# A one-core transformer kernel: the attention output bias as one early row, and the first queries placed ahead of the last down products

## The chip, the cores and the metric

The kernel is one program on one core of a Trainium2 chip. Its five engines run side by side, each through its own queue in order: TensorE (PE: matmuls, with weight loads PEld overlapping them), VectorE (DVE), ScalarE (ACT), GpSimd (POOL) and SyncE (SP, which here only issues DMAs). They wait for each other by semaphores. The metric is the device time of one launch in microseconds (us), lower is better; ratios are taken on the median of several runs.

## What is computed

Two layers on x of 8 batches x 256 tokens x 256 columns, each an attention and a mixture of experts, with residual sums between (L0_xattn mixes the top 2 of 64 context rows; L0_ffn, the first experts, has 16 routed ones, top 4, and a shared one, 96 wide; L1_xattn has 16 heads over 64 context rows; L1_ffn, the second experts, has 8 of width 704, top 2). The last two lines are what the change touches of L1_xattn, with v_img = ctx @ Wv_img + bv_img; the text part of the context is empty here:

```
x = x + L0_xattn(layernorm(x))
x = x + L0_ffn(layernorm(x))
x = x + L1_xattn(layernorm(x))
x = x + L1_ffn(layernorm(x))

q = rms_norm(x @ Wq + bq, gq)
out = attend(q, k_img, v_img) @ Wo + bo
```

The value bias bv is carried past the softmax and added with bo as one row `bv @ Wo + bo`, the same for all tokens: this is "the bias row" below.

## The kernel before

Rows of x stay on the chip in `x_sb` (16 tiles of 128 tokens, two tiles to a batch). Everything is written out by hand: each engine's block lists its instructions in the order in which they run, and nothing reorders them.

**First experts.** The 12 chunks of 128 routed hidden columns and a 13th chunk of 96 shared ones (C0 = 13) are done for four groups of 512 tokens (NG = 4). For a chunk PE makes gate and up products into PSUM banks 0/1 and 2/3 (`up0`, each float32 product as three products of high and low parts, lines 1034 to 1036), ACT takes Silu of the gate (772), DVE multiplies it with the up part (1530, semaphore `b_prod`), multiplies by the tokens' routing weight out of bank 4 (1535, `b_mult`; not for the shared chunk), splits the result into a high part (1540) and a low part (1544, `b_hidden`), and PE makes the down products of the chunk into banks 6 and 7 (`down0`, 12 products for a group, `b_down`). PE runs one chunk ahead: the up products of chunk c+1 stand before the down products of chunk c. After the last group there is nothing to stand ahead, and `down0(NG - 1, C0 - 1, 1)` follows directly on the chunk before. DVE then adds banks 6 and 7 to `x_sb` (1522, `x_new`) and makes the layer norm of the batches 6 and 7: statistics (1329 to 1339), the power of -0.5 on POOL (501), and the normed rows (1350, `ln_rows`). The batches 0 to 5 were normed, turned and copied to `xnT` inside the expert loop already.

**Bias row.** SP issues the load of bo, spread over 128 partitions (`bo_rows`, 128 KB), at line 410, behind its wait for the last down products. PE adds bv @ Wo (1131, two products) and identity @ bo_rows (1132) in bank 4; ACT copies the sum back into `bo_rows` (789, `bo_ready`); POOL adds it to all of `x_sb` (591), one batch at a time.

**Queries.** For each batch b PE makes x @ Wq (1110, four matmuls, eight records in the profile, since each float32 product runs as two), ACT writes the squares and the biased queries (796, 798), and PE sums the squares over columns (1118, `squares`, into bank 7). PE does batch 0, batch 1 and the squares of 0, then turns the normed rows of the batches 6 and 7 (906), which ACT copies (680), and then a loop does the batches 2 to 7. After it DVE scales the sums (1562), POOL takes their power (595), and attention begins (scores 1151, maxima 1567, difference 1575, exponential 819).

SP's queue behind line 410 holds the loads of the second experts' weights, 18 MB (413 and 421), which are first used some 150 us later.

```python
            for n in range(2):
                sp.wait_ge(hi_out[n], 16 * (NPART // 2))
                sp.wait_ge(lo_out[n], 16 * (NPART // 2))
            sp.dma_start(bo_rows, bo1_in.partition_broadcast(P)).then_inc(in_bo, 16)
```

Of the kernel before, what the change touches and what calls it, by code (L numbers as in the profile page):

```python
# [15 lines left out]
ACT = mybir.ActivationFunctionType  # L16
AX = mybir.AxisListType

P = 128
B, S, D = 8, 256, 256  # L20
# [6 lines left out]
C0 = E0 * I0 // P + 1  # L27
# [31 lines left out]
def program(nc, x_in, ctx_in, ctxT_in, itok_in, descT_in, wq0_in, bq0_in, rw0_in, ebias_in,  # L59
            gu0_in, dn0_in, wq1_in, bq1_in, gq1_in, wk1_in, bk1_in, gk1_in, wv1_in, bv1_in,  # L60
            wo1_in, bo1_in, wg1_in, wexp_in, out_rows):
    with ExitStack() as st:
# [38 lines left out]
        arena = sb("arena", [P, 4224])  # L101

        def view(tensor, first, *shape):
            v = tensor[:, first:first + int(np.prod(shape))]
            names = "abcd"[:len(shape)]
            if len(shape) > 1:
                v = v.rearrange(f"p ({' '.join(names)}) -> p {' '.join(names)}",
                                **dict(zip(names[:-1], shape)))
            return v

        xnT = view(xmem, 0, KD, NT * P)
# [41 lines left out]
        kbd = view(wexp, last, 2, KD * HALF)  # L153
        pT = view(wexp, last + 2048, 2, 8, P)
        bo_rows = view(wexp, last + 4096, D)

        xn = view(arena, 0, 2, TB, D)
        xn2 = view(arena, 2560, 2, TB, D)
# [17 lines left out]
        sqT = view(arena, 1024, 2, KD, S)  # L176
# [34 lines left out]
        ident = sb("ident", [P, P])  # L211
        identb = sb("identb", [P, P], BF16)
        ones = sb("ones", [P, P])
# [17 lines left out]
        wq1 = sb("wq1", [P, KD, D])  # L231
# [31 lines left out]
        def bank(i, n=1):  # L263
            return ps[:, 512 * i:512 * (i + n)]
# [9 lines left out]
        b_high, b_low, b_max, b_mult = sem("b_high"), sem("b_low"), sem("b_max"), sem("b_mult")  # L274
        b_prod, b_routed, b_sig, b_silu = sem("b_prod"), sem("b_routed"), sem("b_sig"), sem("b_silu")
# [24 lines left out]
        in_bo, in_ctx, in_exp0, in_exp7 = sem("in_bo"), sem("in_ctx"), sem("in_exp0"), sem("in_exp7")  # L300
        in_gu, in_dn, in_route = [sem("in_gu0"), sem("in_gu1")], sem("in_dn"), sem("in_route")
        in_itok, in_kv, in_rest = sem("in_itok"), sem("in_kv"), sem("in_rest")
# [11 lines left out]
        bo_sum, bo_ready = sem("bo_sum"), sem("bo_ready")  # L314
# [4 lines left out]
        x_new = sem("x_new")  # L319
# [17 lines left out]
        XA, XB, XC = NT, NT + NT // 2, 2 * NT + NT // 2  # L337
        NG = NT // 4
# [17 lines left out]
        def _(sp):  # L356
# [20 lines left out]
            sp.dma_start(wq1[:, :, :], wq1_in.rearrange("(k p) n -> p k n", p=P)).then_inc(in_rest, 16)  # L377
            sp.dma_start(wo1[:, :, :], wo1_in.rearrange("(k p) n -> p k n", p=P)).then_inc(in_rest, 16)
            sp.dma_start(wg1[:, :, :], wg1_in.rearrange("(k p) n -> p k n", p=P)).then_inc(in_rest, 16)

            xn_v = xn_rows.rearrange("(t p) d -> p t d", p=P)
            sp.wait_ge(pool_fill, 1)
# [24 lines left out]
            for n in range(2):  # L407
                sp.wait_ge(hi_out[n], 16 * (NPART // 2))
                sp.wait_ge(lo_out[n], 16 * (NPART // 2))
            sp.dma_start(bo_rows, bo1_in.partition_broadcast(P)).then_inc(in_bo, 16)  # L410
            for e in range(7):
                whole = slice(e * WE, (e + 1) * WE - D)
                sp.dma_start(w_hi[:, whole].bitcast(F32), w_hi_rows[:, whole]).then_inc(in_exp0, 16)
# [262 lines left out]
        def _(act):  # L676
# [107 lines left out]
            for g in range(NG):  # L784
                silu_group(g, g)

            act.wait_ge(in_rest, 16 * 3)
            act.wait_ge(bo_sum, 1)
            act.activation(bo_rows, bank(4)[:, 0:D], ACT.Copy).then_inc(bo_ready, 1)

            def queries(b, k):
                act.wait_ge(c_q, b + 1)
                if k >= 2:
                    act.wait_ge(c_ssq, b - 1)
                for m in range(KD):
                    act.activation(sqT[:, k % 2, m, :], bank(2 + k % 2)[:, m * S:(m + 1) * S], ACT.Square,
                                   bias=vecs[:, 0, m:m + 1]).then_inc(c_sq, 1)
                    act.activation(xnT[:, m, bass.ds(b * S, S)], bank(2 + k % 2)[:, m * S:(m + 1) * S],
                                   ACT.Identity, bias=vecs[:, 0, m:m + 1]).then_inc(c_qT, 1)
            for b in range(2):  # L800
                queries(b, b)
            for b in range(B - 2, B):
                copy_batch(2, b, 0)
            with act.Fori(1, B // 2) as pair:
# [87 lines left out]
        def _(pe):  # L892
# [22 lines left out]
            for m in range(KD):  # L915
                for k in range(KD):
                    pe.matmul(bank(6)[:, m * NK:(m + 1) * NK], wq0[:, k, m * P:(m + 1) * P], descT[:, k, :],
                              start=(k == 0), stop=(k == KD - 1))
            for k in range(KD):
                mm = pe.matmul(bank(6)[0:1, 256:256 + NK], bq0[:, k:k + 1], descT[:, k, :],  # L920
                               start=(k == 0), stop=(k == KD - 1))
# [66 lines left out]
            for m in range(KD):  # L988
                for k in range(KD):
                    mm = pe.matmul(bank(6 + m), wkv[:, k, 0, m * P:(m + 1) * P], ctxT[:, k, :, 0, :],  # L990
                                   start=(k == 0), stop=(k == KD - 1))
# [62 lines left out]
            def down0(g, c, k):  # L1054

                i, rows = g * C0 + c, P if c < C0 - 1 else I0
                if c == 0 and k:
                    pe.wait_ge(x_new, g * 2 + XA)
                if k == 0 and c in (0, 4, 7, 10):
                    pe.wait_ge(dn_low_ready, (0, 4, 7, 10).index(c) + 1)  # L1060
                for j in range(4):
                    if j % 2 == 0:
                        pe.wait_ge(b_hidden, i * 2 + 1 + j // 2)
                    cols = slice(j * P, (j + 1) * P)
                    mm = in_parts(bank(6, 2)[:, j * D:(j + 1) * D], h_high[0:rows, c % 2, cols], h_low[0:rows, c % 2, cols],
                                  dn_high[0:rows, c, :], dn_low[0:rows, c, :], c == 0 and j % 2 == 0, c == C0 - 1)
                mm.then_inc(b_down, 1)
# [29 lines left out]
            pe.wait_ge(b_low, B)  # L1097
            with pe.Fori(1, NG) as g:
                ffn0_group(g, 1)
            down0(NG - 1, C0 - 1, 1)  # L1100

            def queries(b, k):
                pe.wait_ge(ln_copied, 2 * B + b + 1)
                if k >= 2:
                    pe.wait_ge(c_qT, (b - 1) * KD)
                for m in range(KD):
                    for h in range(KD):
                        mm = pe.matmul(bank(2 + k % 2)[:, m * S:(m + 1) * S], wq1[:, h, m * P:(m + 1) * P],  # L1110
                                       xnT[:, h, bass.ds(b * S, S)], start=(h == 0), stop=(h == KD - 1))
                mm.then_inc(c_q, 1)

            def squares(b, k):
                pe.wait_ge(c_sq, b * KD + KD)
                for j in range(TB):
                    for m in range(KD):
                        mm = pe.matmul(bank(7)[:, bass.ds(b * TB + j, 1)], sqT[:, k % 2, m, j * P:(j + 1) * P],
                                       ones[:, 0:1], start=(m == 0), stop=(m == KD - 1))
                mm.then_inc(c_ssq, 1)  # L1120

            def queries_squares(b, k):
                queries(b, k)
                if k == 1:
                    pe.wait_ge(x_new, XB)
                if k >= 1:
                    squares(b - 1, k - 1)
            pe.wait_ge(in_rest, 16 * 3)
            pe.wait_ge(in_bo, 16)
            for k in range(KD):  # L1130
                pe.matmul(bank(4)[:, 0:D], vecs[:, 4, k:k + 1].broadcast_to([P, P]), wo1[:, k, :], start=(k == 0), stop=False)
            pe.matmul(bank(4)[:, 0:D], ident[:, :], bo_rows, start=False, stop=True).then_inc(bo_sum, 1)
            for b in range(2):
                queries_squares(b, b)
            for b in range(B - 2, B):
                turn_rows(2, b, b % 2)
            with pe.Fori(1, B // 2) as pair:
# [678 lines left out]
```

## Time and profile before

| | |
|---|---|
| median of 3 runs | 782.27 us (781.16 to 784.03) |
| profiled execution, its own time | 782.75 us |
| its span, first to last instruction | 781.0 us |
| mean granted TensorE clock | 0.929 of full speed |
| busy: PE / DVE / POOL / ACT | 700.1 / 476.0 / 328.7 / 259.1 us |
| chain of waits that ends last, by engine | PE 75%, DVE 15%, issue 4%, ACT 2%, DMA 1% |

The span is 1.75 us shorter than the time of the same execution. PE is busy nearly throughout, so the places where it stands still, and those where its clock is at half, are the ones to read. Times in a timeline are microseconds from the start of the span. A row of the timeline may merge several instructions (x8); the square brackets give how long the engine had been idle before it and who ended that.

### The profile page before, as it was taken

What the parts mean: (1) busy time and instruction counts of PE and PEld (TensorE: products, weight loads), DVE (VectorE), ACT (ScalarE), POOL (GpSimd) and SP (SyncE); (2) the same over time, 40 slices, a digit from 0 to 9 for tenths busy, and PEclk for the clock granted to TensorE, in tenths of its full rate; (3) what the DMA queues carried; (4) which work ended last, traced back from release to release, by engine and by line L of the source; (5) the groups of instructions that cost most, each with busy time, mean ns of one, the idle gap of its engine ahead of it and who ended that gap; (6) DMA issues with size and microseconds to landing.
All of it is one profiled execution on the core that took longest, in us unless ns stands there. A gap on an engine that the chain in (4) does not pass through costs nothing.

```text
span 781.0 us, 14817 instructions
## 1 busy us (share of the span) xinstructions
PE 700.1 (90%) x4735; PEld 623.7 (80%) x4735; DVE 476.0 (61%) x1326; ACT 259.1 (33%) x491; POOL 328.7 (42%) x318
## 2 busy tenths in 40 slices
PE   4799479999999999969799992699999999999996
PEld 4668368878878878858677772589999999999996
DVE  5959956667667768760399956644444444444443
ACT  1356133222223222314567740022222222222221
POOL 6136933334334434426212115235555545455542
PEclk9786679999999999988899995599999999999998
DMA  8801046766666666559900008422254345525221
GB/s 223 312 1 53 3 139 221 246 210 221 225 233 203 216 231 225 196 169 427 337 12 32 29 29 272 160 78 41 43 156 114 77 149 157 151 48 156 43 35 21
DMA packets 60407, 115.08 MB, mean 147 GB/s; under 512 B 15200, under 2 KB 29536, under 8 KB 57920
## 3 DMA queue, kind: packets, MB, share of 16 engines
q1 hardware_dynamic: 50656, 103.61, 38.8%
q0 software_dynamic: 8736, 10.39, 8.0%
q8 instruction: 37, 0.61, 0.3%
q10 hardware_dynamic: 960, 0.33, 0.2%
q14 instruction: 18, 0.15, 0.1%
HBM read 69.02 MB, written 45.29 MB: 146 GB/s over the span
## 4 chain that ended last, share of the span: by engine, by line
PE 75%; DVE 15%; issue 4%; ACT 2%; DMA 1%; another core or an unknown queue 1%; POOLq 0%; POOL 0%; DVEq 0%; ACTq 0%
PE ps L1034 18%; PE ps L1036 17%; PE ps L1035 17%; PE ps L1277 3%; PE ps L1151 2%; PE ps L1160 2%; PE ps L1110 2%; PE ps L1197 2%; PE ps L1077 1%; DVE h_high L1540 1%; DVE h_low L1544 1%; PE ps L1173 1%; PE ps L906 1%; PE ps L1256 1%; DVE arena L1350 1%
## 5 line engine op out<-in xcount | busy, mean ns | idle before, releaser
L561 POOL TENSOR_TENSOR part_lo<-wexp,part_hi 128x512 fp32r<-128x512 f32 x68 | 89.4, 1324 | 133.5 <-ACT part_hi L783 127.1
L650 POOL DMA_INDIRECT out_rows<-vbd,slot_row x39 | 62.9, 1613 | 109.3 <-DVE vbd L1731 77.1
L1034 PE MATMUL ps<-w_hi,x_high 128*128 x312 | 104.4, 335 | 1.1 <-DVE x_low L1736 1.1
L1036 PE MATMUL ps<-w_hi,x_low 128*128 x312 | 101.0, 324 | 0.0
L1035 PE MATMUL ps<-up_low,x_high 128*128 x312 | 100.9, 324 | 0.0
L1752 DVE TENSOR_TENSOR arena<-arena,ps 128x704 f32<-128x704 f32 x39 | 34.6, 887 | 103.9 <-ACT arena L874 76.7
L1034 PE MATMUL ps<-xn_high,gu_high 128*128 (+3 forms) x208 | 92.5, 445 | 0.1
L772 ACT ACTIVATE wexp<-ps 128x512 f32<-128x512 f32 (+1 forms) x52 | 31.1, 599 | 160.2 <-PE ps L1036 160.2
L1035 PE MATMUL ps<-xn_low,gu_high 128*128 (+3 forms) x208 | 82.2, 395 | 0.0
L1036 PE MATMUL ps<-xn_high,gu_low 128*128 (+3 forms) x208 | 82.2, 395 | 0.0
L501 POOL TENSOR_TENSOR rstd<-ve,mhalf 128x2 f32<-128x2 f32 (+1 forms) x32 | 22.8, 713 | 115.3 <-DVE ve L1339 115.3
L874 ACT ACTIVATE arena<-ps 128x704 f32<-128x704 f32 x39 | 29.6, 760 | 120.8 <-PE ps L1036 65.1
L1034 PE MATMUL ps<-dn_high,h_high 128*128 128x256 f32 (+1 forms) x208 | 61.5, 296 | 7.2 <-DVE h_low L1544 7.2
L1034 PE MATMUL ps<-w_hi,hT_high 128*128 x195 | 58.8, 302 | 2.0 <-DVE hT_high L1745 2.0
L1034 PEld LDWEIGHTS ps<-w_hi,x_high 128*128 128x128 f32 x312 | 59.3, 190 | 1.5 <-issue 1.5
L1035 PEld LDWEIGHTS ps<-up_low,x_high 128*128 128x128 f32 x312 | 59.2, 190 | 0.0
L1530 DVE TENSOR_TENSOR wexp<-wexp,ps 128x512 f32<-128x512 f32 (+1 forms) x52 | 35.6, 685 | 38.6 <-ACT wexp L772 38.5
L1036 PEld LDWEIGHTS ps<-w_hi,x_low 128*128 128x128 f32 x312 | 59.0, 189 | 0.0
L1035 PE MATMUL ps<-dn_low,h_high 128*128 128x256 f32 (+1 forms) x208 | 59.0, 284 | 0.0
L1036 PE MATMUL ps<-dn_high,h_low 128*128 128x256 f32 (+1 forms) x208 | 58.8, 283 | 0.0
L1544 DVE TENSOR_TENSOR h_low<-wexp,h_high 128x256 fp32r<-128x256 f32 (+1 forms) x104 | 55.4, 573 | 1.8
L1036 PE MATMUL ps<-w_hi,hT_low 128*128 x195 | 55.7, 286 | 0.0
(274 smaller groups left out, 1700.2 us busy)
## 6 DMA issues: line engine op xcount, KB each, us to landing
wexp<-in_wexp SPq DMA_DIRECT2D x68, 256.0 KB, 3.2
w_hi_rows<-part_hi SPq DMA_DIRECT2D x68, 256.0 KB, 2.5
w_lo_rows<-part_lo SPq DMA_DIRECT2D x68, 256.0 KB, 2.1
w_hi<-w_hi_rows SPq DMA_DIRECT2D x8, 2048.0 KB, 20.2
up_low<-w_lo_rows SPq DMA_DIRECT2D x8, 1408.0 KB, 6.2
down_low<-w_lo_rows SPq DMA_DIRECT2D x8, 768.0 KB, 8.6
wexp<-in_gu SPq DMA_DIRECT2D x2, 1632.0 KB, 10.6
xn_rows<-arena SPq DMA_DIRECT2D x8, 256.0 KB, 2.1
```

What stands on the lines that cost most here:

```text
L501: pool.tensor_tensor(rstd[:, bass.ds(b * TB, TB)], ve[:, bass.ds(b * TB, TB)], mhalf[:, 0:1].broadcast_to([P, TB]), ALU.pow).then_inc(ln_r ...
L561: pool.tensor_tensor(part_lo[:, n % 2, :], part_w[:, n % 4, :], part_hi[:, n % 2, :].bitcast(F32), ALU.subtract).then_inc(p_lo, 1)
L650: pool.indirect_dma_start(out=out_rows, out_offset=bass.IndirectOffsetOnAxis(ap=slot_row[:, i:i + 1], axis=0), in_=yb[:, i % 2, :], in_off ...
L772: act.activation(sg0[0:rows, c % 2, :], bank(c % 2)[0:rows, :], ACT.Silu).then_inc(b_silu, 1)
L874: act.activation(sg1.rearrange("p (a n) -> p a n", a=2), bank(0, 2).rearrange("p (a n) -> p a n", a=2)[:, :, 0:HALF1], ACT.Silu).then_inc( ...
L1034: pe.matmul(out, high, rows_high, start=start, stop=False, skip_group_check=True)
L1035: pe.matmul(out, high, rows_low, start=False, stop=False, skip_group_check=True)
L1036: return pe.matmul(out, low, rows_high, start=False, stop=stop, skip_group_check=True)
L1277: mm = pe.transpose(bank(4, 2)[:, c * P:(c + 1) * P], h1[:, c * P:(c + 1) * P], ident[:, :])
L1530: dve.tensor_tensor(hm0[0:rows_, c % 2, :], sg0[0:rows_, c % 2, :], bank(2 + c % 2)[0:rows_, :], ALU.mult).then_inc(b_prod, 1)
L1544: dve.tensor_tensor(h_low[0:rows_, c % 2, cols], hm0[0:rows_, c % 2, cols], h_high[0:rows_, c % 2, cols].bitcast(F32), ALU.subtract).then_ ...
L1752: dve.tensor_tensor(h1[:, 0:I1].rearrange("p (a n) -> p a n", a=2), sg1.rearrange("p (a n) -> p a n", a=2), bank(2, 2).rearrange("p (a n) ...
```

## The change

It has four parts. (1) bo is loaded as one row of 1 KB into partition 96 of `arena`, near the start of SP's queue, and the 128 KB load at line 410 is gone. (2) The product of the identity with `bo_rows` becomes a product of one row of ones with `bo_row`, contracted over that single partition. (3) On PE, the queries of batch 0 and the bias products stand ahead of the last down products, and the queries of batch 1 behind them; the two PSUM banks of the queries are swapped (`3 - k % 2`), so that the queries of batch 0 go to bank 3, which the chunk before the last has left. (4) On ACT the copy of the bias row stands between the queries of batch 0 and those of batch 1.

```diff
+        bo_row = arena[96:97, 1792:1792 + D]
...
             sp.dma_start(wg1[:, :, :], wg1_in.rearrange("(k p) n -> p k n", p=P)).then_inc(in_rest, 16)
+            sp.dma_start(bo_row, bo1_in.unsqueeze(0)).then_inc(in_bo, 16)
...
-            sp.dma_start(bo_rows, bo1_in.partition_broadcast(P)).then_inc(in_bo, 16)
...
-            act.wait_ge(in_rest, 16 * 3)
-            act.wait_ge(bo_sum, 1)
-            act.activation(bo_rows, bank(4)[:, 0:D], ACT.Copy).then_inc(bo_ready, 1)
-
...
-                    act.activation(sqT[:, k % 2, m, :], bank(2 + k % 2)[:, m * S:(m + 1) * S], ACT.Square,
+                    act.activation(sqT[:, k % 2, m, :], bank(3 - k % 2)[:, m * S:(m + 1) * S], ACT.Square,
...
-            for b in range(2):
-                queries(b, b)
+            queries(0, 0)
+            act.wait_ge(bo_sum, 1)
+            act.activation(bo_rows, bank(4)[:, 0:D], ACT.Copy).then_inc(bo_ready, 1)
+            queries(1, 1)
...
             with pe.Fori(1, NG) as g:
                 ffn0_group(g, 1)
-            down0(NG - 1, C0 - 1, 1)
...
             pe.wait_ge(in_rest, 16 * 3)
+            pe.wait_ge(b_prod, NG * C0 - 1)
+            queries(0, 0)
             pe.wait_ge(in_bo, 16)
+            pe.wait_ge(b_mult, NG * (C0 - 1))
             for k in range(KD):
                 pe.matmul(bank(4)[:, 0:D], vecs[:, 4, k:k + 1].broadcast_to([P, P]), wo1[:, k, :], start=(k == 0), stop=False)
-            pe.matmul(bank(4)[:, 0:D], ident[:, :], bo_rows, start=False, stop=True).then_inc(bo_sum, 1)
-            for b in range(2):
-                queries_squares(b, b)
+            pe.matmul(bank(4)[:, 0:D], ones[96:97, :], bo_row, start=False, stop=True).then_inc(bo_sum, 1)
+            down0(NG - 1, C0 - 1, 1)
+            pe.wait_ge(b_prod, NG * C0)
+            queries(1, 1)
+            pe.wait_ge(x_new, XB)
+            squares(0, 0)
```

TensorE's queue at the end of the first experts' loop, before (the branch of line 1098 closes the loop; the first three and last three of the 12 down products are those of 1034 to 1036 in their order):

```order
L1098 COMPARE_AND_BRANCH
L1034 MATMUL ps<-dn_high,h_high 128x256 [waits b_hidden]
...
L1036 MATMUL ps<-dn_high,h_low 128x256
L1131 MATMUL ps<-wo1,vecs 128x256 [waits in_bo,in_rest]
L1131 MATMUL ps<-wo1,vecs 128x256
L1132 MATMUL ps<-wexp,ident 128x256
L1110 MATMUL ps<-xmem,wq1 128x256 [waits ln_copied]
...
L1118 MATMUL ps<-ones,arena 128x1 [waits c_sq,x_new]
```

The same place after the change (its line numbers are one or two lower):

```order
L1097 COMPARE_AND_BRANCH
L1108 MATMUL ps<-xmem,wq1 128x256 [waits ln_copied,b_prod,in_rest]
L1108 MATMUL ps<-xmem,wq1 128x256 x3
L1129 MATMUL ps<-wo1,vecs 128x256 [waits b_mult,in_bo]
L1129 MATMUL ps<-wo1,vecs 128x256
L1130 MATMUL ps<-arena,ones 128x256
L1033 MATMUL ps<-dn_high,h_high 128x256 [waits b_hidden]
...
L1035 MATMUL ps<-dn_high,h_low 128x256
L1108 MATMUL ps<-xmem,wq1 128x256 [waits ln_copied,b_prod]
L1108 MATMUL ps<-xmem,wq1 128x256 x3
L1116 MATMUL ps<-ones,arena 128x1 [waits c_sq,x_new]
```

Four query products and three bias products now stand between the loop and the last 12 down products; four query products moved behind those; the turns of the batches 6 and 7 and the loop over the other queries follow as before.

## Rows read from the trace of the kernel before

**Rows 1.** Chain of waits, 344 to 363 us: start, length, what (all in us).
```profile
344.07 0.43 DVE h_low L1544
344.50 0.04 issue
344.55 0.39 PE ps L1034
...
346.60 0.23 PE ps L1036
346.82 0.02 issue
346.84 4.15 DMA wexp<-in_bo
350.99 0.14 issue
351.12 2.04 PE ps L1131 x4
353.17 0.85 PE ps L1132 x2
354.02 4.33 PE ps L1110 x16
```

**Rows 2.** Timeline of TensorE, 342 to 364 us: start, length, instruction, idle before.
```profile
342.57 0.28 PE L1036 MATMUL ps<-dn_high,h_low 128*128 128x256 f32 x1
344.55 0.39 PE L1034 MATMUL ps<-dn_high,h_high 96*128 96x256 f32 x1 [1.69 <-DVE h_low L1544]
...
360.57 0.63 PE L906 MATMUL ps<-ident,arena 128*128 128x128 f32 x4 [0.96 <-ACT xmem L680]
361.04 1.95 PE L1110 MATMUL ps<-xmem,wq 128*128 x8
362.82 0.95 PE L1118 MATMUL ps<-ones,arena 128*128 128x1 f32 x8
363.63 1.97 PE L1110 MATMUL ps<-xmem,wq 128*128 x8
```

**Rows 3.** Timeline of TensorE, attention: a projection at full clock, scores and turns.
```profile
378.36 1.13 PE L1151 MATMUL ps<-wexp,arena 64*128 64x256 f32 x8
382.17 2.08 PE L1151 MATMUL ps<-wexp,arena 64*128 64x256 f32 x8 [2.68 <-DVE arena L1575]
384.20 1.97 PE L1160 MATMUL ps<-ident,arena 128*128 128x128 f32 x8
...
395.10 1.03 PE L1197 MATMUL ps<-wo,wexp 128*128 128x256 f32 x4
```

**Rows 4.** Timeline of VectorE, 346 to 379 us.
```profile
346.85 1.28 DVE L1522 TENSOR_TENSOR x_sb<-x_sb,ps 128x512 f32<-128x512 f32 x2 [2.02 <-PE ps L1036]
...
350.61 0.73 DVE L1350 TENSOR_SCALAR arena<-x_sb,mean,rstd 128x256 f32<-128x256 f32 x2
351.60 1.31 DVE L1350 TENSOR_SCALAR arena<-x_sb,mean,rstd 128x256 f32<-128x256 f32 x2 [0.27 <-POOL rstd L501]
378.47 0.17 DVE L1562 TENSOR_SCALAR ssq<-ps 128x16 f32<-128x16 f32 x1 [25.55 <-PE ps L1118]
```

**Rows 5.** Windows, half a us and one us each: PE, PEld, DVE, ACT, POOL busy, then PEclk.
```profile
345.00:345.50 0.50, 0.50 (x6) 0.50 (x5) 0.00 (x0) 0.00 (x0) 0.00 (x0) 0.90 0.61 225
355.50:356.00 0.50, 0.50 (x3) 0.44 (x2) 0.00 (x0) 0.00 (x0) 0.50 (x1) 0.86 1.15 492
379.50:380.00 0.50, 0.00 (x0) 0.00 (x0) 0.46 (x1) 0.00 (x0) 0.50 (x1) 0.53 1.00 426
386.00:386.50 0.50, 0.17 (x1) 0.00 (x0) 0.50 (x1) 0.29 (x1) 0.00 (x0) 0.64 1.11 229
65.00:66.00 1.00, 1.00 (x5) 0.85 (x5) 1.00 (x4) 1.00 (x2) 0.57 (x1) 0.75 0.00 0
79.00:80.00 1.00, 1.00 (x11) 1.00 (x11) 1.00 (x2) 0.84 (x2) 1.00 (x2) 0.92 0.00 0
```

**Rows 6.** Timeline of GpSimd, 351 to 382 us.
```profile
351.54 2.42 POOL L575 TENSOR_TENSOR wexp<-kT,gmask 128x256 f32<-128x256 f32 x4
354.86 9.84 POOL L591 TENSOR_TENSOR x_sb<-x_sb,wexp 128x512 f32 x8 [0.90 <-ACT wexp L789]
378.72 2.91 POOL L595 TENSOR_TENSOR rq<-ssq,mhalf 128x16 f32<-128x16 f32 x1 [14.02 <-DVE ssq L1562]
```

**Rows 7.** SyncE's DMA issues, 21 to 351 us.
```profile
21.13 0.87 SPq L379 DMA_DIRECT2D wg<-in_wg  x1
...
73.49 1.76 SPq L393 DMA_DIRECT2D wexp<-in_wexp  x4
...
347.21 3.80 SPq L413 DMA_DIRECT2D w_hi<-w_hi_rows  x7
```

**Rows 8.** Timeline of ScalarE, 354 to 358 us.
```profile
354.12 0.38 ACT L789 ACTIVATE wexp<-ps 128x256 f32<-128x256 f32 x1 [11.70 <-PE ps L1132]
356.65 0.47 ACT L796 ACTIVATE arena<-ps,vecs 128x256 f32<-128x256 f32 x1 [2.14 <-PE ps L1110]
```

More of the change, by code:

```diff
@@ L795, in queries @@
                 for m in range(KD):
-                    act.activation(sqT[:, k % 2, m, :], bank(2 + k % 2)[:, m * S:(m + 1) * S], ACT.Square,
+                    act.activation(sqT[:, k % 2, m, :], bank(3 - k % 2)[:, m * S:(m + 1) * S], ACT.Square,
                                    bias=vecs[:, 0, m:m + 1]).then_inc(c_sq, 1)
-                    act.activation(xnT[:, m, bass.ds(b * S, S)], bank(2 + k % 2)[:, m * S:(m + 1) * S],
+                    act.activation(xnT[:, m, bass.ds(b * S, S)], bank(3 - k % 2)[:, m * S:(m + 1) * S],
                                    ACT.Identity, bias=vecs[:, 0, m:m + 1]).then_inc(c_qT, 1)
-            for b in range(2):
-                queries(b, b)
+            queries(0, 0)
+            act.wait_ge(bo_sum, 1)
+            act.activation(bo_rows, bank(4)[:, 0:D], ACT.Copy).then_inc(bo_ready, 1)
+            queries(1, 1)
             for b in range(B - 2, B):
@@ L1109, in queries @@
                     for h in range(KD):
-                        mm = pe.matmul(bank(2 + k % 2)[:, m * S:(m + 1) * S], wq1[:, h, m * P:(m + 1) * P],
+                        mm = pe.matmul(bank(3 - k % 2)[:, m * S:(m + 1) * S], wq1[:, h, m * P:(m + 1) * P],
                                        xnT[:, h, bass.ds(b * S, S)], start=(h == 0), stop=(h == KD - 1))
@@ L1123, in queries_squares @@
                 queries(b, k)
[L1124 to L1127, printed above, removed]
+                squares(b - 1, k - 1)
             pe.wait_ge(in_rest, 16 * 3)
+            pe.wait_ge(b_prod, NG * C0 - 1)
+            queries(0, 0)
             pe.wait_ge(in_bo, 16)
+            pe.wait_ge(b_mult, NG * (C0 - 1))
             for k in range(KD):
                 pe.matmul(bank(4)[:, 0:D], vecs[:, 4, k:k + 1].broadcast_to([P, P]), wo1[:, k, :], start=(k == 0), stop=False)
-            pe.matmul(bank(4)[:, 0:D], ident[:, :], bo_rows, start=False, stop=True).then_inc(bo_sum, 1)
-            for b in range(2):
-                queries_squares(b, b)
+            pe.matmul(bank(4)[:, 0:D], ones[96:97, :], bo_row, start=False, stop=True).then_inc(bo_sum, 1)
[4 more added lines that the diff above has]
+            squares(0, 0)
             for b in range(B - 2, B):
```

## The prediction

> **What bounds the kernel now.** I read the chain of waits first. In the stretch that the change touches it runs on TensorE except at two spots [rows 1]: the last down products start at 344.55 when DVE has the low part of the shared chunk, and after them the chain is a DMA of 4.15 us, the load of bo that SP issues only when those products are done. Then come the bias products, 2.04 and 0.85 us, and the queries. The timeline of TensorE shows the same as idle time [rows 2]: 1.69 us before the last down products, 0.96 us before the second turn of rows. The bo load leaves PE idle from 346.80 to 351.12, 4.32 us. The windows give the third thing to see [rows 5]: the granted clock falls from full (2.4 GHz) to half (1.2 GHz) inside the window at 345.0 (a mean of 0.90 over half a us puts it at 345.4), and is full again from 355.64 (0.86 in the window at 355.5). So the bias products and part of the first queries ran at half: 16 query records took 4.33 us [rows 1], where 8 take 1.81 us at full clock (362.82 less 361.04, or 363.63 plus 1.83 by the chain, [rows 2]).
>
> Behind this stretch nothing else waits to take the place of PE: DVE stood 25.55 us for the sums of squares [rows 4] and POOL 14.02 us after its bias additions [rows 6]. From 361.04 on, PE runs queries and squares back to back, so the start of the loop over the batches 2 to 7 at 361.04 is the point to measure at: what it moves, the end moves, apart from clock effects.
>
> **The change, part by part.** Before, from the issue of the last product of the chunk before (342.57, the next could go 0.12 later at 342.69) to 361.04 there are 18.35 us. I build the same stretch anew.
>
> 1. *Queries of batch 0* start at 342.69: their inputs are turned rows copied long ago, and the bank was read by DVE for chunk 11 before. At full clock 1.81 us [rows 2]: to 344.50. ACT squares and biases them meanwhile (0.47 us an activation, [rows 8]); it was idle there anyway, 11.70 us [rows 8].
>
> 2. *Bias products.* Bank 4's last reader is DVE's routing product of chunk 11, done before the down products of that chunk, which PE has issued by then. The two wo1 products are four records; the nearest row is the projection with the same weights' size, 1.03 us for four with the last one's tail [rows 3]. The next record could start before that tail ends, so I take 0.9. The one-row product has the same 128 weight columns and 256 moving columns as the identity product it replaces, which took 0.85 us at half clock [rows 1], so 0.43 at full. Bounds: nothing, if a single row were free, and 0.85. Together 1.3: to 345.8. Their DMA wait is gone: the row is asked for behind the load at 21.13, and SP's first issue that anything here needs is at 73.49 [rows 7]; one issue more (0.87 us at most in that row) is covered by tens of us. If that cover were gone it would cost those 0.87 us.
>
> 3. *Last down products.* Their operand is ready at 344.5 [rows 1], so PE comes 1.3 us late to them. But the clock should hold at full over them, since PE no longer stands for 1.69 us: 12 products in 1.5 us instead of 2.25 (346.80 less 344.55). They end at 347.5, **0.7 us later** than before. DVE, and through it POOL and the turns, are that much later: this is the price of the change.
>
> 4. *Queries of batch 1, squares of batch 0*: 1.8 and 0.8 us [rows 2], to 350.0; the additions on x that the squares wait for take 1.28 us from 347.5 [rows 4], so they are in time.
>
> 5. *Turns of the batches 6 and 7.* What is late next is DVE's layer norm. It ends the rows of batch 6 at 351.34 and those of batch 7 at 352.91 [rows 4]; with the 0.7 us they come at 352.0 and 353.6. PE waits about 2.0 us for the first and 1.1 for the second, then turns (0.47 us, 361.04 less 360.57): the loop starts at 354.1. **361.04 less 354.1 is 6.9 us** at full clock throughout.
>
> 6. *The clock.* PE has little to do from 349.2 to 353.6: sums of squares (one moving column each), waits and one turn. Before, the clock fell after a stand of 1.69 us, and after the attention's first scores with a stand of 2.68 us [rows 2, 3]. I take it that it falls here too. It came back 4.5 us after steady work resumed at 351.12 (355.64), and 4.2 after 382.17 (386.36, from the 0.64) [rows 1, 3, 5]; I use 4.35. Counted from the first turn (352.0) it would be back at 356.35, and from 353.6 on 2.7 us would run at half, which costs half of that, about 1.3; counted from 353.6, it would be back at 357.95, and the cost is 2.2. Bounds: 0 (no fall) and that 2.2. I take 1.7, between the two readings. **Gain 6.9 - 1.7 = 5.2 us.**
>
> 7. *POOL*: its bias additions began at 354.86 and took 9.84 us [rows 6]. They no longer wait 0.90 us for ACT, but the products with the mask ahead of them start 0.7 later, at 352.2, and end at 354.7; so they end at 364.5, as before. The power at line 595 needs the squares, then at about 373: 8 us of cover. Costed at nothing. *SP*: the weight loads start 0.35 us later (0.7 later, one issue fewer in front, [rows 7]) and nobody waits for them for 150 us: nothing.
>
> 8. *Loop exit on PE.* What the branch out of the expert loop costs is not visible, since 1.69 us of waiting cover it. Bounds 0 and 1.69. I take 0: where PE goes from one pass of the query loop to the next there is no idle time (362.82 plus 0.95 reaches past 363.63, [rows 2]).
>
> The sum is made against the profiled execution: 782.75 - 5.2 = **777.6 us**. That execution lies 0.5 us above the median of 782.27, so against the median the gain would be 4.7.
>
> At step 6 a rule of the skill speaks for another outcome. The trace shows that 1.69 us of standing were followed by half clock [rows 2, 5]. The Trainium skill, "TensorE: Matmul & The Clock Gate", section "Why this matters for your kernels", names a fall in mid-kernel only for idle gaps longer than either of the two that I expect here. By that rule the clock would hold, the sum would lose nothing at step 6, and the time would be 775.9; the row at 345.0 disagrees with it here.
>
> **The rivals.**
>
> *A. The clock holds and the whole gain comes through.* The two stands of 2.0 and 1.1 us are separated by a turn, and PE is never without work for as long as the 4.32 us of before. Against it stands the fall after 1.69 us. 782.75 - 6.9 = 775.9. This is also what the skill's rule above gives. If moreover the attention's first scores and turns fell outside half clock (2.08 and 1.97 against 1.1 us each, [rows 3]), 1.9 more: 774.0. Chance 0.2.
>
> *B. Part of the gain is eaten.* Either the loop exit of step 8 shows with up to 1.69 us (779.3), or the clock falls earlier at the attention's entry, so that the eight score records of 378.36 also take 2.08 instead of 1.13 us (+0.95) on top of a cost of 2.2 at step 6 (779.1). For it: entry into attention comes in another clock phase than before. Chance 0.15.
>
> *C. The wait is only handed on.* The change does its work but PE waits for DVE as long as it waited for the DMA; this needs the rows of batch 7 at about 360 instead of 353.6. The rows say 352.91 [rows 4] and leave no such wait. 782 us. Chance 0.05.
>
> *D. Slower: the clock falls at about 352 and does not come back in the query loop.* Before, that loop was entered at full clock; now it would be entered at half. Place: the loop's six batches, 1.83 us of query records each at full, 11.0 us, doubled, so +11 us, and up to 0.8 us each for the squares, so +11 to +16. Less 6.9: 787 to 792 us. It decides from the point where half clock lasts more than 14 us from 353.6. For it: from 65.5 to 79.2 the clock stayed at half for 13.7 us with PE busy all the time, in work with many short products [rows 5]. Against it: twice it came back 4.2 and 4.5 us after work resumed, under float32 products of 256 columns, which is what the loop mostly holds. Chance 0.05.
>
> **How the numbers follow.** My forecast has 0.55, A 0.2, B 0.15, C 0.05, D 0.05. A change of 0.5%, 3.9 us, is about what a measurement of this kernel can tell from none; the bound lies at 778.4. The forecast lies 0.8 us inside it, and since three runs spread over 2.9 us I give it 0.45 of its 0.55 on the faster side; with A's 0.2 and a little of B this is 0.68 for faster, 0.27 for within 0.5% (the rest of the forecast, most of B, C), 0.05 for slower. The range goes from 774.9 (half way into A's deeper case) to 780.4 (B with both of its costs, 1.69 and 0.95, on the forecast is 780.2); C and D are outside.
>
> **What would show it.** In the profile after: no wait for a DMA at the bias products and none of 1.69 us before the last down products; these 12 in about 1.5 us, ending near 347.5; two waits of PE of about 2.0 and 1.1 us for DVE's normed rows (and ACT's copy of batch 6); the query loop starting near 354 to 355 instead of 361.04; the clock at half from about 352 to 356 to 358. ACT's copy of the bias row moves from 354.12 to about 346; POOL's bias additions still end near 364.6. The prediction is wrong if the loop starts before 353 or after 356, if a wait stands at the loop's exit, or if the difference at the loop's start is not found again at the end.

## The result and the profile after

Over 20 runs of each the change takes 778.48 us (median, 772.71 to 782.16) and the kernel before 783.50 us (779.38 to 785.53). The ratio is **0.9939, 95% interval 0.9923 to 0.9955**: faster by 0.6%. The medians are 5.0 us apart. The forecast was 777.6, with a gain of 5.2 on the profiled execution; by the profiled executions themselves the gain is 3.3 (table).

| | before | after |
|---|---|---|
| median of 20 runs, us | 783.50 | 778.48 |
| profiled execution: its time / its span, us | 782.75 / 781.0 | 779.47 / 777.7 |
| mean granted TensorE clock | 0.929 | 0.937 |
| busy PE / DVE / POOL / ACT, us | 700.1 / 476.0 / 328.7 / 259.1 | 705.9 / 476.4 / 328.4 / 259.2 |

The chain of waits after the change, from the last products before the new place of the queries (start, length, what; compare [rows 1]):

```profile
342.95 1.73 PE ps L1108 x8
344.67 0.86 PE ps L1129 x4
345.54 0.62 PE ps L1130 x2
...
347.82 1.29 DVE x_sb L1523 x2
...
351.91 0.42 DVE arena L1351
...
352.37 1.13 PE ps L905 x4
...
353.52 0.61 ACT xmem L681
...
354.27 1.09 PE ps L905 x4
355.36 3.41 PE ps L1108 x8
```

The DMA of 4.15 us is gone from it. In its place the chain now runs through DVE, from its addition at 347.82 to the first normed rows of batch 6, done at 352.33: 4.5 us. TensorE's timeline shows the stands (answers to [rows 2]):

```profile
342.67 0.28 PE L1035 MATMUL ps<-dn_high,h_low 128*128 128x256 f32 x1
342.79 1.89 PE L1108 MATMUL ps<-xmem,wq 128*128 128x256 f32 x8
344.51 1.03 PE L1129 MATMUL ps<-wo,vecs 128*128 128x256 f32 x4
345.47 0.69 PE L1130 MATMUL ps<-arena,ones 1*128 1x256 f32 x2
346.09 0.38 PE L1033 MATMUL ps<-dn_high,h_high 96*128 96x256 f32 x1
...
352.37 1.11 PE L905 MATMUL ps<-ident,arena 128*128 128x128 f32 x4 [2.07 <-DVE arena L1351]
354.27 1.09 PE L905 MATMUL ps<-ident,arena 128*128 128x128 f32 x4 [0.78 <-ACT xmem L681]
355.15 3.62 PE L1108 MATMUL ps<-xmem,wq 128*128 x8
...
359.64 1.97 PE L1108 MATMUL ps<-xmem,wq 128*128 x8
...
374.37 1.13 PE L1152 MATMUL ps<-wexp,arena 64*128 64x256 f32 x8
...
392.57 1.03 PE L1198 MATMUL ps<-wo,wexp 128*128 128x256 f32 x4
```

No stand before the last down products, two new ones of 2.07 and 0.78 us behind them, and a first loop batch of 3.62 us against 1.97 for the next: half clock. The windows place the clock (columns as in [rows 5]):

```profile
352.00:352.50 0.50, 0.13 (x1) 0.13 (x2) 0.32 (x1) 0.00 (x0) 0.50 (x1) 0.79 0.56 229
359.00:359.50 0.50, 0.50 (x5) 0.50 (x5) 0.00 (x0) 0.50 (x2) 0.50 (x1) 0.88 1.16 492
376.00:376.50 0.50, 0.00 (x0) 0.00 (x0) 0.50 (x1) 0.00 (x0) 0.50 (x1) 0.69 1.15 492
386.00:386.50 0.50, 0.50 (x4) 0.41 (x4) 0.25 (x1) 0.00 (x0) 0.00 (x0) 0.57 1.07 184
```

From the means in column PEclk it fell at 352.3 and was back at 359.1, and fell again at 376.2, at the entry into attention, to be back at 386.4. Before, those two stretches were 345.4 to 355.6 and 379.5 to 386.4.

A measure for all runs below: **S**, from the issue of the last down product of chunk 11 (342.57 in [rows 2]) to the first attention scores (378.36 in [rows 3]). Before, S is 35.79 us. After, it is 374.37 - 342.67 = 31.70. The change took 4.1 us out of this stretch in the profiled executions. S has the advantage that it leaves out where executions already differ when they reach this place: the same product was issued at 342.57 to 342.67 in four of the profiled executions of this study and at 344.45 to 344.75 in the other eight.

S also leaves out the entry into attention, where the clock falls and returns, and that is a weakness: what a kernel saves before it can be lost there. So the table has a second measure, **T**, from the same product to the first projection of attention (395.10 in [rows 3], 392.57 after). T is 52.53 us before and 49.90 after: of the 4.1 us of S, 1.5 are lost again at the entry, since the half clock there lasted 10.2 us (376.2 to 386.4) instead of 6.8 (379.5 to 386.4). Both measures are of one execution each, and the ratios decide.

### The profile page after: what moved, and what is told of

The parts are those of the page before. It is cut to its first block, busy times and chain, and to the rows that moved or that the text cites. A ratio compares the mean times of both kernels' runs of the same rounds, so it can differ in the third digit from the quotient of the medians.

```text
span 777.7 us, 14818 instructions
## 1 busy us (share of the span) xinstructions
PE 705.9 (91%) x4735; PEld 628.9 (81%) x4735; DVE 476.4 (61%) x1326; ACT 259.2 (33%) x491; POOL 328.4 (42%) x318
## 4 chain that ended last, share of the span: by engine, by line
PE 76%; DVE 16%; issue 4%; ACT 2%; DMA 1%; POOLq 0%; POOL 0%; DVEq 0%; ACTq 0%
PE ps L1033 18%; PE ps L1034 17%; PE ps L1035 17%; PE ps L1278 3%; PE ps L1152 2%; PE ps L1161 2%; PE ps L1108 2%; PE ps L1198 2%; PE ps L1076 1%; PE ps L905 1%; PE ps L1174 1%; PE ps L1257 1%; DVE h_low L1545 1%; DVE arena L1351 1%; DVE h_high L1541 1%
```

## The experiments

All kernels of the study carry one maximum on TensorE's wait for the low weight parts of the second experts. It lies behind the stretches read here, and costs little there: behind the first projection of attention, 385.1 us are left in the change and 385.2 with the maximum. Ratios are to the kernel before on the same chip; c0, e1, e2 and e3 ran on one chip, e4 to e7 on a second, e8 and e9 on a third. Medians in us are compared directly only within one of these groups; across them the ratios are the fair comparison.

| kernel | median us | ratio (95%) | S, us | T, us |
|---|---|---|---|---|
| before | 782.3 to 784.0 | 1 | 35.79 | 52.53 |
| change | 778.48 | 0.9939 (0.9923 to 0.9955) | 31.70 | 49.90 |
| c0, change with the maximum | 779.65 | 0.9957 (0.9932 to 0.9982) | 31.66 | 49.83 |
| e1, early row alone | 779.38 | 0.9962 (0.9945 to 0.9979) | 28.83 | 48.25 |
| e2, order alone, late load | 777.75 | 0.9936 (0.9910 to 0.9962) | 31.35 | 48.10 |
| e3, bias products behind queries 1 | 776.43 | 0.9916 (0.9887 to 0.9944) | 29.16 | 45.94 |
| e4, stands filled with unread products | 777.60 | 0.9920 (0.9889 to 0.9951) | 29.10 | 48.49 |
| e5, e3 with batches 2 and 3 ahead | 776.26 | 0.9910 (0.9883 to 0.9937) | 27.14 | 45.72 |
| e6, e3 with down products first | 777.11 | 0.9921 (0.9890 to 0.9951) | 28.74 | 45.55 |
| e7, e5 with attention's entry filled | 773.05 | 0.9873 (0.9846 to 0.9900) | 27.13 | 42.99 |
| e8, e7 with down products first | 776.80 | 0.9928 (0.9903 to 0.9953) | 30.50 | 46.37 |
| e9, e7 with one-row products as filling | 777.22 | 0.9937 (0.9915 to 0.9958) | 27.10 | 48.92 |

Behind the projection the profiled executions have 385.1 to 385.9 us left, but 384.5 in e5, 384.1 in e8, 382.7 in e2 and 382.5 in e9; what shortens it there stays open.

### c0: the base of the study

```diff
-                        nc.s_assert_within(landed, 32, 32 * E1, skip_runtime_bounds_check_because=why))
+                        smax(landed, 32))
```

> The changed kernel, with one maximum per expert block on TensorE's wait for the low weight parts (all kernels of this study carry it). Nothing else differs, so every theory expects the ratio of the change, 0.994 (0.992 to 0.996); what it lies above that is the price of the maximum, which is then in all the others too.

0.9957 with an interval that holds 0.9939; S is 31.66 against 31.70 and the same product rows, stands and half clock. So c0 stands for the change, with a shift in the ratio that these runs cannot tell from none. Its profiled execution, 781.54 us, lies 1.9 us above its median.

### e1: the early row alone

```diff
+            sp.dma_start(bo_row, bo1_in.unsqueeze(0)).then_inc(in_bo, 16)
...
-            sp.dma_start(bo_rows, bo1_in.partition_broadcast(P)).then_inc(in_bo, 16)
...
-            pe.matmul(bank(4)[:, 0:D], ident[:, :], bo_rows, start=False, stop=True).then_inc(bo_sum, 1)
+            pe.matmul(bank(4)[:, 0:D], ones[96:97, :], bo_row, start=False, stop=True).then_inc(bo_sum, 1)
```

> Only the early one-row load and the one-row product; TensorE's and ScalarE's order is that of before. My theory: the stand of 4.3 us goes, the bias products start at 346.8 at half clock, and with rows of batch 7 at 352.9 the query loop starts at about 356.7, 4.3 us earlier, at full clock: ratio 0.9945, nearly all that the change brings. Rival, the order is what counts (the stretch behind the down products is then bound by the half clock and the queries): the loop starts at 359 or later, ratio 0.998 or above.

0.9962 against c0's 0.9957: the medians are 0.3 us apart. The new order, as the change has it, adds nothing that these runs can show (by the intervals up to 2 us could hide). The theory's 0.9945 is at the edge of e1's interval, the rival's 0.998 outside. TensorE's timeline of e1:

```profile
346.43 0.39 PE L1036 MATMUL ps<-dn_high,h_high 96*128 96x256 f32 x1 [1.69 <-DVE h_low L1546]
...
347.96 1.03 PE L1133 MATMUL ps<-wo,vecs 128*128 128x256 f32 x4
348.92 0.69 PE L1134 MATMUL ps<-arena,ones 1*128 1x256 f32 x2
349.54 3.72 PE L1112 MATMUL ps<-xmem,wq 128*128 128x256 f32 x16
...
355.50 0.63 PE L908 MATMUL ps<-ident,arena 128*128 128x128 f32 x4 [0.95 <-ACT xmem L682]
355.96 1.95 PE L1112 MATMUL ps<-xmem,wq 128*128 x8
```

The stand of 1.69 us is still there, but behind it TensorE has the bias products and both query batches to do while DVE norms, and stands only 0.95 us for a copy. In this execution the clock stayed full until 373.6, through the stand of 1.69 us, so S is even 2.8 us below c0's. The half clock at attention's entry then lasted 13.7 us (to 387.2), and in T 1.6 us of the 2.8 are left; the medians, 0.3 us apart, show neither. The forecast for e1 said that the bias products would run at half clock; here they ran at full. The same stand was followed by half clock in the kernel before and not in e1 or in e6: in which executions it is cannot be read off from these profiles, and it stays open.

### e2: the order alone

(against the kernel before)

```diff
+            pe.wait_ge(b_prod, NG * C0 - 1)
+            queries(0, 0)
+            down0(NG - 1, C0 - 1, 1)
+            pe.wait_ge(b_prod, NG * C0)
+            queries(1, 1)
+            pe.wait_ge(x_new, XB)
+            squares(0, 0)
             pe.wait_ge(in_bo, 16)
...
             pe.matmul(bank(4)[:, 0:D], ident[:, :], bo_rows, start=False, stop=True).then_inc(bo_sum, 1)
```

> Queries of batch 0 ahead of the last down products and those of batch 1 behind them, but the bias is loaded late as 128 KB as before, and its products stand behind the first squares. My theory: the down products are 1.4 us earlier than in the change, the load lands at about 350.5 while TensorE would wait for normed rows anyway, and the loop starts at 353.5 to 355: ratio 0.991 to 0.995, as good as the change. Rival, the early load is essential: the loop starts at 358 or later, ratio 0.998.

0.9936, and S 31.35, which is as good as the change (theory: 0.991 to 0.995; the rival's 0.998 is outside the interval). The load is as late as before, and its wait is hidden for the most part:

```profile
350.00 0.95 PE L1117 MATMUL ps<-ones,arena 128*128 128x1 f32 x8
352.69 1.24 PE L1135 MATMUL ps<-wo,vecs 128*128 128x256 f32 x4 [1.73 <-DMA wexp<-in_bo]
```

So each half of the change alone is as good as both, as far as these runs can tell: the 4.32 us of [rows 2] can be removed by an earlier load or, for the most part, by work put in front of the products that need it. That there is more to gain with the bias products in another place, e3 shows.

### e3: the bias products behind the queries of batch 1

```diff
-        bo_row = arena[96:97, 1792:1792 + D]
+        bo_row = arena[96:97, 2048:2048 + D]
...
+            down0(NG - 1, C0 - 1, 1)
+            pe.wait_ge(b_prod, NG * C0)
+            queries(1, 1)
             pe.wait_ge(in_bo, 16)
...
             pe.matmul(bank(4)[:, 0:D], ones[96:97, :], bo_row, start=False, stop=True).then_inc(bo_sum, 1)
-            down0(NG - 1, C0 - 1, 1)
-            pe.wait_ge(b_prod, NG * C0)
-            queries(1, 1)
```

On ACT the copy of the bias row follows the queries of batch 1.

> The change, with the three bias products moved from before the last down products to behind the queries of batch 1 (the row lies elsewhere in the arena). My theory: the bias products before the down products delay DVE's layer norm by 1.5 us, and behind the queries they fill a stand instead; loop start 1.3 us earlier than in the change, and with stands of 0.6 and 1.0 us left the clock may hold, 1.7 more: ratio 0.990 to 0.993. Rival, the delay is hidden by something else (ACT's copies, POOL): the ratio of the change, 0.994.

0.9916, 3.2 us below c0 in the median, S 2.5 us less and T 3.9 less. The down products start 1.99 us behind the last one of chunk 11, where they start 3.42 behind it in the change, and the stands are smaller:

```profile
352.99 0.66 PE L906 MATMUL ps<-ident,arena 128*128 128x128 f32 x4 [0.39 <-DVE arena L1352]
354.56 1.11 PE L906 MATMUL ps<-ident,arena 128*128 128x128 f32 x4 [0.92 <-DVE arena L1352]
```

This shows what the place of the bias products in the change costs: they delay DVE, which is the longer chain. The ratio lies in the range of the theory (0.990 to 0.993). The clock did not hold, though: it was at half from 354.3 to 357.8, 3.4 us instead of the change's 6.8. All eight runs of e3 (773.00 to 777.93) are below all twelve of e1 (778.25 to 781.61), so the early row with its products behind the queries brings more than the early row alone; by e6, further down, the queries of batch 0 ahead have no measurable part in that. By S and T against e2 (31.35 and 48.10), which has nearly the same order, the early one-row load is worth 2.2 us, and 1.3 in the median, where the runs of the two overlap.

### e4: the stands filled

```diff
             squares(0, 0)
-            for b in range(B - 2, B):
-                turn_rows(2, b, b % 2)
+            for n in range(4):
+                pe.matmul(bank(1)[:, 0:D], ident[:, :], wq1[:, n % KD, :], start=True, stop=True)
+            turn_rows(2, B - 2, 0)
+            pe.matmul(bank(1)[:, 0:D], ident[:, :], wq1[:, 0, :], start=True, stop=True)
+            turn_rows(2, B - 1, 1)
```

> The change, with five float32 products of 128x256 that nobody reads on TensorE: four in front of the turn of batch 6 and one between the two turns. They fill the stands of 2.1 and 0.8 us and do no work. My theory: the half clock behind those stands costs about 2 us, and with them filled the clock stays full through the query loop (first batch 1.9 us instead of 3.6): 1 to 2 us less than the guarded change, ratio 0.993 to 0.995. Rival, the stands themselves are the whole cost, or the clock falls anyway: ratio of the guarded change, 0.9957, or 0.5 us above it for the added products.

S falls from 31.66 to 29.10, by products that do no work:

```profile
354.23 0.65 PE L906 MATMUL ps<-ident,arena 128*128 128x128 f32 x4 [0.24 <-DVE arena L1355]
354.72 0.60 PE L1140 MATMUL ps<-wq,ident 128*128 128x256 f32 x2
355.81 0.66 PE L906 MATMUL ps<-ident,arena 128*128 128x128 f32 x4 [0.49 <-DVE arena L1355]
356.30 1.91 PE L1109 MATMUL ps<-xmem,wq 128*128 x8
```

The windows of e4, columns as before:

```profile
352.00:356.30 4.30, 3.57 (x20) 2.62 (x20) 3.38 (x15) 1.57 (x4) 3.38 (x6) 1.00 1.01 423
356.30:373.00 16.70, 16.19 (x102) 14.87 (x100) 0.00 (x0) 10.05 (x26) 10.29 (x9) 1.00 1.00 428
```

The clock is 1.00 in both. The turns take 0.65 instead of 1.1 us and the first loop batch 1.9 instead of 3.6. The first turn starts 9.71 us behind chunk 11's last product in both, so the added products delay nothing and only the clock differs: 2.6 us is what the half clock behind the two stands cost in S. It did not all reach the end. The clock fell at 373.5, as attention began, and stayed at half for 13.7 us (10.2 in c0), and in T 1.3 us of the 2.6 are left. The ratio, 0.9920 (0.9889 to 0.9951), is below the 0.993 to 0.995 of the theory and points the same way, though its interval overlaps c0's.

### e6: the queries of batch 0 back behind the down products

```diff
-            pe.wait_ge(b_prod, NG * C0 - 1)
-            queries(0, 0)
             down0(NG - 1, C0 - 1, 1)
             pe.wait_ge(b_prod, NG * C0)
+            queries(0, 0)
             queries(1, 1)
```

(against e3)

> e3, with the queries of batch 0 behind the last down products: the stand of 1.7 us before these is back, everything else as in e3. My theory: DVE's layer norm sets the start of the turns, so moving 1.8 us of queries in front is worth only about 1 us: ratio 0.992 to 0.994. Rival, the queries ahead are worth all their 1.8 us and hold the clock too: ratio 0.995 or more.

0.9921 against e3's 0.9916, S 28.74 against 29.16. The median is 0.7 us above e3's, within the intervals, and S is 0.4 us below: e3's execution had the clock at half from 354.3 to 357.8, e6's not before 374. With the stand of 1.8 us back, nothing measurable is lost (T 45.55 against 45.94). e6 differs from e1 mainly in where the bias products stand, behind the queries instead of in front: S is the same within 0.1 us, T is 2.7 us less, and the ratios are 0.9921 and 0.9962 with intervals that just overlap. In T the half clock at attention's entry counts, 6.8 us instead of 13.7; why it was shorter stays open. My theory had 1 us, its ratio of 0.992 to 0.994 was met, and the rival's 0.995 was not.

### e5 and e7: batches 2 and 3 ahead, and attention's entry filled

```diff
+            for b in range(2, 4):
+                queries_squares(b, b)
             for b in range(B - 2, B):
                 turn_rows(2, b, b % 2)
-            with pe.Fori(1, B // 2) as pair:
+            with pe.Fori(2, B // 2) as pair:
...
                     scores(t, t)
+                for n in range({0: 6, 1: 2}.get(t, 0)):
+                    pe.matmul(bank(6)[:, 0:D], ident[:, :], wq1[:, n % KD, :], start=True, stop=True)
```

The first hunk, with the same on ACT, is e5 (on e3); both together are e7.

> e3, with queries and squares of the batches 2 and 3 also ahead of the turns of 6 and 7 (two passes fewer in the loop). My theory: TensorE has work for the whole time in which DVE norms the batches 6 and 7, no stand over 0.5 us is left between the expert loop and the last squares, and the clock holds: attention begins 3 us earlier than in e3, ratio 0.987 to 0.989. Rival, POOL's bias additions (9.8 us from about 353) or ACT become the bound: ratio of e3, 0.9916.

> e5, with unread products also at the entry into attention: six behind the first scores and two behind the second, where TensorE stands 2.7 us for DVE. My theory: the fall of the clock there costs 2 to 3 us (scores and turns at 2.0 instead of 1.1 us), and filling holds it: ratio 0.984 to 0.986. Rival, entry is bound by POOL's power and ACT's table load whatever the clock: ratio of e5 or up to 0.001 above it.

e5 has S 27.14, 2.0 us less than e3, but its ratio of 0.9910 is no lower than e3's beyond the interval; I had expected 3 us and 0.987 to 0.989. T shows where it went: it is only 0.2 us less than e3's, since the half clock at attention's entry lasted 10.2 us instead of 6.8. One stand of 0.95 us for ACT's copy is left between the turns. POOL's additions, rival to this, ran from 355.26 to 365.1 and POOL then stood 6.86 us: no bound. e7 holds the clock at 1.00 from 342 to 400, and the second scores and the turns behind them take half the time of [rows 3]:

```profile
369.80 1.13 PE L1157 MATMUL ps<-wexp,arena 64*128 64x256 f32 x8
370.86 2.86 PE L1218 MATMUL ps<-wq,ident 128*128 128x256 f32 x12
373.65 1.13 PE L1157 MATMUL ps<-wexp,arena 64*128 64x256 f32 x8
374.71 1.13 PE L1218 MATMUL ps<-wq,ident 128*128 128x256 f32 x4
375.68 1.05 PE L1166 MATMUL ps<-ident,arena 128*128 128x128 f32 x8
```

0.9873 (0.9846 to 0.9900), 3.2 us below e5 in the median: **the fastest kernel of the study, 773.05 us**, the last 3.2 us by 16 records that nobody reads. The whole gain, 1.3%, is about twice that of the change. The theory's 0.984 to 0.986 is a little lower, within the interval; the rival's 0.991 to 0.992 is outside. T is 2.7 us less than e5's. e7's runs lie at 772.19 to 775.19, e5's at 774.61 to 777.75.

### e8: is the order worth something where TensorE is the bound?

The edit is that of e6, on e7.

> e7 with the queries of batch 0 behind the last down products, as before the change: none of the change's new order on TensorE is left in it, only the early row, the bias products behind the queries of batch 1, the batches 2 and 3 ahead of the turns, and the unread products at the entry into attention. My theory, after e3 against e6 showed nothing: the queries ahead are worth at most 0.3 us while the layer norm sets the turns, but here TensorE's own work sets the end of the stretch, so the stand of 1.7 us should now show: 1.0 to 1.7 us above e7, ratio 0.9885 to 0.9895. Rival, the order ahead is worth nothing anywhere: ratio of e7, 0.987.

0.9928 against 0.9873, with intervals that do not touch: about 4 us more, by the ratios since the two ran on different chips. S is 30.50 against 27.13 and T 46.37 against 42.99, 3.4 us more in both. Here the order matters, and by more than the stand of 1.8 us and than the 1.0 to 1.7 of my theory (TensorE's timeline of e8):

```profile
346.62 0.35 PE L1036 MATMUL ps<-dn_high,h_high 96*128 96x256 f32 x1 [1.79 <-DVE h_low L1551]
...
348.83 4.51 PE L1111 MATMUL ps<-xmem,wq 128*128 128x256 f32 x16
```

And its windows:

```profile
347.00:347.50 0.50, 0.50 (x5) 0.50 (x5) 0.00 (x0) 0.00 (x0) 0.00 (x0) 0.72 0.59 217
350.50:351.00 0.50, 0.50 (x3) 0.43 (x2) 0.50 (x2) 0.00 (x0) 0.00 (x0) 0.87 0.19 66
```

The clock fell at 347.2 behind the stand, with down products and queries at half until 350.6. Of the 3.4 us in S, 1.7 are the half clock (3.4 us of it, in which half the time is lost) and the other 1.7 the stand.

### e9: what a one-row product costs, and whether it holds the clock

```diff
-                    pe.matmul(bank(6)[:, 0:D], ident[:, :], wq1[:, n % KD, :], start=True, stop=True)
+                    pe.matmul(bank(6)[:, 0:D], ones[96:97, :], bo_row, start=True, stop=True)
```

> e7 with its eight unread products made as the change makes the bias row: ones of one partition times a row, 128x256, float32. It measures the one-row product by itself (0.62 to 0.69 us for its two records in the change, against my 0.43). My theory: 0.43 us each in a row like those with 128 partitions, the excess in the change being a start of its own; and, since only one of 128 rows of the array works, I leave open whether they hold the clock: if they do, ratio of e7, 0.987, and scores in 1.1 us; if not, ratio of e5, 0.991, and scores in 2.08 us.

TensorE's timeline of e9, and the first seven of the twelve records by themselves:

```profile
370.83 3.64 PE L1218 MATMUL ps<-arena,ones 1*128 1x256 f32 x12
374.40 2.08 PE L1157 MATMUL ps<-wexp,arena 64*128 64x256 f32 x8
...
370.83 1.77 PE L1218 MATMUL ps<-arena,ones 1*128 1x256 f32 x7
```

The window in which the clock fell:

```profile
372.50:373.00 0.50, 0.50 (x4) 0.38 (x3) 0.50 (x1) 0.00 (x0) 0.50 (x1) 0.76 0.92 393
```

The second case came: the clock fell at 372.8 in the midst of the one-row products, where with 128-row products of the same number of columns it held (e7, and e8 too), and the scores took 2.08 us. TensorE was busy in both by the busy column. These are three executions; the ratio, 0.9937 against e7's 0.9873 with intervals that do not touch, says that the loss is in the other runs too. It is even above e5's 0.991: S, which ends before the filling, is that of e7, but T is 3.2 us more than with no filling at all (e5), since at half clock the added products themselves are late. From the first scores to the turns behind the second ones it takes 8.64 us here and 5.84 in e5. The price: seven records in 1.77 us at full clock, of which the last one's own length is 0.37 (the shortest of the 16), leave 1.40 us for six, 0.23 each. That is the rate of 128-row products (0.96 us for four in the change), so a product of two records takes 0.47 in a row, near my 0.43, and the 0.62 us in the change (346.09 less 345.47) hold a start of its own.

## Why the prediction was right, and where a step was off

The time, the direction, the place of the two new stands and the clock's fall came as forecast. Two terms were mis-sized, the cost of the clock above all, one loss was not in the sum, and the gain is owed to less of the change than the working let appear. That the median came so near the forecast all the same is partly luck.

1. *Queries of batch 0*: from 342.79 to 344.51, 1.72 us for the forecast 1.81. (The difference that the working gives for it, 362.82 less 361.04, is 1.78.)
2. *Bias products*: 1.58 us (344.51 to 346.09) for 1.3. The two wo1 products took 0.96, the one-row product 0.62 instead of 0.43: this term was mis-sized by 0.2, the other by 0.06.
3. *Down products*: they start 3.42 us behind chunk 11's last (1.98 before, 3.2 forecast), run at full clock as forecast (1.70 us with the tail; 2.25 before), and end at 347.79, for 347.5. The working's own terms, 345.8 and 1.5, make 347.3; it is with the measured 1.70 that they make 347.5. DVE's addition is 0.9 us later from the reference point instead of 0.7. e3 shows that without the bias products in front the gain would have been larger.
4. *Stands*: forecast 2.0 and 1.1 us, measured 2.07 and 0.78. The second was released by ACT's copy (353.52 to 354.12), not by DVE's rows (ready at 353.90), because the first turn already ran at half clock and took 1.13 us.
5. *Clock*: fall at 352.3 (forecast 352), return at 359.1, for 356.35 to 357.95. I had counted 4.35 us from the first or second turn; it took 4.9 from the second. **This is the term that was mis-sized**: 1.7 us in the sum, with 2.2 as its bound, and 2.6 by e4. Without it the sum holds: it had 6.9 us at full clock, and e4, at full clock, has S 6.7 us below before. The loop started at 355.15 instead of 354.1 and its next batch was 4.0 us earlier than before (359.64 against 363.63), where the sum gave 5.2.
6. *Attention's entry* was not in the sum: the working took it that what the loop's start moves, the end moves. Of the 4.1 us at the first scores, 1.5 were lost at the entry (T: 2.6 us left), since the half clock there reached from 376.2 to 386.4. This is rival B's second mechanism, the half clock laid otherwise over attention's entry, though in another place than B put it: the first scores took 1.13 us as before, and the instructions behind the second scores ran at half for longer. Its price was above B's 0.95. Behind the projection 0.8 us came back (385.9 against 385.1 left).
7. *POOL, SP, loop exit* were costed at nothing, rightly: the bias additions ran to 364.7 (forecast 364.5), attention's POOL instruction then waited 10.0 us, and the first query follows 0.12 us behind the loop's last product.

The medians are nevertheless 5.0 us apart, near the 5.2. By the times of the profiled pair, 782.75 and 779.47, the gain was 3.3; the sum was made for such a pair, so it missed there by 1.9 us, and the agreement with the medians is partly luck. Among the change's 20 runs five lie at 772.7 to 775.5 and the others from 777.3 up; no run of before's 20 is under 779.38. Which clock stretches the five avoided isn't known, since none of them was profiled.

*The rivals.* A, the whole gain with the clock held, did not occur in the profiled executions. The clock fell behind stands of 2.07 us (change, where eight products of one column had run for 0.95 us right before the stand) and 1.79 us (e8, with full products on both sides). The Trainium skill ("TensorE: Matmul & The Clock Gate", "Why this matters for your kernels") names such a fall only for idle gaps above about 3 us; here shorter ones were followed by it, so the traces do not bear that bound out. B's second mechanism occurred (step 6), its first did not. C, a wait handed on, occurred only in the part that the working had priced: of the stands of 1.69, 4.32 and 0.96 us before, 6.97 together, 2.85 us for DVE and ACT were left, for a forecast of 3.1. D did not occur.

What the prediction did not see is that parts 1 and 3 of the change, as it makes them, are alternatives. It built one sum for the whole. A second sum, with the early row alone, would have given a loop start of 356.7 at full clock (the expectation of e1) against 354.1 plus 1.7 us of half clock, 355.8: 0.9 us between them. e1's measured ratio then showed no difference beyond its interval. Nor did it ask where the bias products had better stand: step 3 calls their delay of DVE the price of the change, and e3 shows that the price need not be paid.

## What to carry to other kernels

A wait on a load can be removed by an earlier load or by work in front of its user. Cost the two apart before making both: here the second added nothing that could be measured (e1, e2), and it did matter once the bias products stood elsewhere and the layer norm was covered with work (e7 against e8). Work put ahead of a product that another engine waits for delays that engine's whole chain; put it behind (e3, 3.2 us in the median). Where TensorE stands, price the clock behind the stand as well: 2.6 us for two stands of 2.9 us together (e4), 1.7 for one of 1.8 (e8). And follow a saving to the next place where the clock moves: half of e4's 2.6 us, and 1.8 of the 2.0 that e5 saved against e3 in S, were gone behind attention's entry.

## What was not expected of the hardware

- **One-row products did not hold the clock.** Twelve records of 1x256 kept PE busy for 3.6 us and it fell to half among them (372.8, e9); with twelve of 128x256 in their place it stayed at full (e7).
- A one-row product among 128-row ones took 0.62 us for its two records at full clock (change), where two of 128 rows take 0.48; in a row of its own kind it takes 0.47 (e9). So contracting over one partition saved nothing here.
- The same stand of 1.69 to 1.79 us before the last down products was followed by half clock in two kernels (before, e8) and not in two others (e1, e6).
- Filling stands with products that nobody reads took 3.2 us off the median of a kernel whose useful work was unchanged (e5 against e7).
